# A Perceiver block with its second cross-attention rebuilt around 32x32 block transposes and row tiles

## The chip, the cores and the metric

The kernel runs on one core of one Trainium2 chip. The metric is the device time of one execution in microseconds (us). A profiled execution gives the trace, whose rows are quoted below: PE is TensorE's matmul side, PEld its weight loads, DVE VectorE, ACT ScalarE, POOL GpSimd, SP SyncE, and "SPq" rows are instructions of SP's own stream, which issues every DMA of this kernel.

## The reference, cut to what matters

Six stages are applied in turn to x of shape 64 x 32 x 128: cross-attention, memory attention, experts, a second cross-attention, a recurrent block and a quantised feed-forward block. The change touches the fourth, and what the third prepares for it:

```python
x = x + _L1_xattn_ref(ctx_1024, _layernorm(x), mask, Wq, Wkv, Wout, bout, g_media, b_media, g_latent, b_latent)

xn = layer_norm(ctx, g_media, b_media)        # 64 x 257 x 128
ln = layer_norm(latents, g_latent, b_latent)  # 64 x 32 x 128
kv_input = concatenate([xn, ln], axis=1)      # 289 keys a batch
sim = einsum('bhqd,bhfd->bhqf', q, k)         # 16 heads, 32 queries
sim = where(mask, max_neg, sim)
out = einsum('bhqf,bhfv->bhqv', softmax(sim), v) @ Wout + bout
```

## The kernel before

All is f32, and tokens lie as columns (128 features on the partitions) unless said otherwise. The weights are folded: `wqk` (16 heads of 128x128) turns a latent into a query that is multiplied with the normed key input itself, and `wvo` takes the mean of key inputs to the output. So the second cross-attention needs, for each of 64 batches, the 289 key inputs once as columns (`keyT`, for the scores) and once as rows (for the means).

**experts_0.** Besides 8 experts on 2048 tokens it norms the context. Its work is a loop of 32 units in 4 turns of 8. In unit s, PE does `up` (4 matmuls of 512 columns, L1085), `turn` of the context tiles of unit s-2 (4 transposes, L1107) and `down` of unit s-1 (16 matmuls, L1094). VectorE does, in this order, `measure` (4 BN_STATS, L1180), `normalise` of the unit before (4 tensor_scalar, L1200), `gather` (4 BN_AGGR, L1189) and, once `down` is made, 4 sums into `acc` (L1219). PE's `turn` waits for `normed`, which `normalise` counts up. SP loads each pair of context batches into a ring of four slots, in 2 DMAs (L1032), when the slot has been turned; ScalarE applies gain and bias while it copies the turned tiles into `keyT` (L1154).

**cross_attention_1.** A unit is one group of 4 heads of one batch: 128 rows (4 heads x 32 queries) by 289 keys; 4 units are a batch, 256 units in all. Per batch SP copies the key columns to a buffer (L1291) and loads the mask row (L1292), and PE turns the key columns into rows with 3 transposes (L1321), which VectorE copies (L1446). Per unit:

```python
nc.tensor.matmul(S[u % 2], q..., key[:, b % 2, 0:KEYS], start=True, stop=False)           # L1344
nc.tensor.matmul(S[u % 2][:, 0:CTX], lowest[:], maskb[:, b % 2, :], start=False, ...)     # L1345
nc.vector.tensor_reduce(nmax..., S[u % 2], AXX, ALU.max, negate=True)                     # L1472
nc.scalar.activation(P..., S[u % 2], ACT.Exp, bias=nmax..., accum_out=total...)           # L1426
nc.vector.tensor_scalar(P..., P..., rtotal..., None, ALU.mult)                            # L1452
nc.tensor.transpose(TP[u % 2]..., P[:, u % 4, ...], core.ident[:])                        # L1353, 3 of them
nc.scalar.activation(pT..., TP[u % 2], ACT.Copy)                                          # L1418
nc.tensor.matmul(OP..., xv[:, b % 2, k, :], pT[:, u % 2, k, :], ...)                      # L1364, k in 0..2
```

The queries of the next four batches (L1331, 16 matmuls, copied by ScalarE at L1411) and the projection of the last four (L1373, 16 matmuls) are spread or placed among the units. An f32 matmul appears in the trace as two passes with a weight load each; a transpose as one pass. A matmul of 4 independent tiles of 32 rows stands in the first cross-attention: its scores (L373) multiply 32 rows by 32 rows for 4 groups of heads, each into a bank of its own. That stage also has the mask and maximum in one VectorE instruction (L470), and the kernel's only 32x32 block transposes (L515).

## Time and profile before

| | us |
|---|---|
| median of 3 runs (lowest, highest) | 1561.96 (1558.83, 1562.1) |
| the profiled execution, own time | 1562.48 |
| its span, first to last instruction | 1560.7 |
| PE busy in the span | 1362.0 |
| VectorE / ScalarE / GpSimd busy | 851.6 / 804.3 / 146.0 |
| mean granted TensorE clock | 0.919 of full speed |

The span is what the trace covers; the profiled execution took 1.78 us more. Busy time is a mean over stages that have different limits, so a stage is read by its own stretch of the trace: the experts' loop from about 464 to 727 us and the second cross-attention from about 754 to 1318 us.

### The profile page before, as it was taken

How to read it: one execution, taken by the hardware profiler on the slowest of the kernel's cores; microseconds unless marked ns; L12 is line 12 of the kernel's file. 1: busy time of each engine (PE TensorE's matmuls, PEld its weight loads, DVE VectorE, ACT ScalarE, POOL GpSimd, SP SyncE). 2: the span in 40 equal slices, each digit the busy share in tenths (PEclk: the TensorE clock that was granted, in tenths of full speed). 3: DMA queues.
4: the chain of work that ended last, by engine and by line, in shares of the span. 5: the costliest groups of instructions: out<-in, count | busy, mean ns of one | idle time of the engine just before them, and what ended most of it. 6: DMA issues, size and time to landing. Idle time of an engine off the chain costs nothing. (4 is left out here: it accounts for less than half of the span.)

```text
span 1560.7 us, 36610 instructions
## 1 busy us (share of the span) xinstructions
PE 1362.0 (87%) x12406; PEld 1038.3 (67%) x12406; DVE 851.6 (55%) x2728; ACT 804.3 (52%) x1838; POOL 146.0 (9%) x432
## 2 busy tenths in 40 slices
PE   5799999666759999997899999999999999577855
PEld 2677777366536777775688888888888887212433
DVE  3466666478433444444555555555555554654387
ACT  3588888278314444442555555455555554444423
POOL 0122221364001111110000000000000000000000
PEclk8899999899669999997999999999999999787965
DMA  3332331000012111110000000000000000000000
GB/s 96 89 75 73 76 74 50 1 0 0 0 52 86 55 55 47 48 41 0 20 17 16 21 15 19 15 19 15 19 15 19 15 21 4 1 0 1 20 1 27
DMA packets 58225, 47.58 MB, mean 30 GB/s; under 512 B 11048, under 2 KB 55600, under 8 KB 58032
## 3 DMA queue, kind: packets, MB, share of 16 engines
q1 hardware_dynamic: 58160, 46.74, 10.9%
q8 instruction: 37, 0.61, 0.2%
q14 instruction: 28, 0.23, 0.0%
HBM read 36.07 MB, written 1.18 MB: 24 GB/s over the span
## 5 line engine op out<-in xcount | busy, mean ns | idle before, releaser
L1426 ACT ACTIVATE d_p<-bank,d_nmax 128x289 f32<-128x289 f32 x256 | 128.8, 503 | 239.0 <-DVE d_nmax L1472 238.9
L1364 PE MATMUL bank<-d_pT,d_xv 128*128 128x128 f32 x1536 | 220.3, 280 | 0.1
L1472 DVE TENSOR_REDUCE d_nmax<-bank 128x1 f32<-128x289 f32 x256 | 116.7, 456 | 171.3 <-PE bank L1345 169.6
L1364 PEld LDWEIGHTS bank<-d_pT,d_xv 128*128 128x128 f32 x1536 | 191.3, 191 | 12.1 <-ACT d_pT L1418 6.3
L1344 PE MATMUL bank<-d_key,d_q 128*128 128x289 f32 x512 | 167.3, 408 | 0.6 <-ACT d_q L1411 0.4
L1162 ACT ACTIVATE c_hs<-bank,c_w 128x512 f32<-128x512 f32 x128 | 87.8, 687 | 147.1 <-PE bank L1085 145.6
L431 ACT ACTIVATE a_p<-a_p,a_nmax 128x257 f32<-128x257 f32 x256 | 115.5, 500 | 38.6 <-DVE a_nmax L470 38.5
L1353 PE MATMUL bank<-ident,d_p 128*128 128x128 f32 x768 | 125.9, 273 | 0.1
L1418 ACT ACTIVATE d_pT<-bank 128x384 f32<-128x384 f32 x256 | 123.0, 480 | 0.9 <-PE bank L1353 0.8
L1085 PE MATMUL bank<-yT,c_w 128*128 128x512 f32 x256 | 118.2, 606 | 6.0 <-DMA c_w<-in_L_ffn_w 6.0
L1094 PE MATMUL bank<-c_w,c_hs 128*128 128x128 f32 x1024 | 122.0, 278 | 0.0
L1094 PEld LDWEIGHTS bank<-c_w,c_hs 128*128 128x128 f32 x1024 | 119.3, 195 | 0.1
L1353 PEld LDWEIGHTS bank<-ident,d_p 128*128 128x128 f32 x768 | 91.4, 141 | 38.2 <-DVE d_p L1452 6.1
L1219 DVE SCALAR_TENSOR_TENSOR c_acc<-bank,c_gates,c_acc 128x128 f32<-128x128 f32 x128 | 36.0, 344 | 142.6 <-PE bank L1094 142.6
L470 DVE CUSTOM_DVE_ANT_0 a_p<-bank,a_low 128x257 f32<-128x257 f32 x256 | 93.6, 422 | 28.1 <-PE bank L373 27.6
L1452 DVE TENSOR_SCALAR d_p<-d_p,d_rtotal 128x289 f32<-128x289 f32 x256 | 95.3, 372 | 9.1
L1085 PEld LDWEIGHTS bank<-yT,c_w 128*128 128x128 f32 x256 | 47.4, 195 | 54.6 <-issue 48.1
L1344 PEld LDWEIGHTS bank<-d_key,d_q 128*128 128x128 f32 x512 | 77.7, 192 | 1.2 <-ACT d_q L1411 0.6
L1331 PE MATMUL bank<-d_latT,x_wqk 128*128 (+1 forms) x512 | 68.6, 279 | 3.8 <-POOL d_lowest L1309 3.8
L1345 PE MATMUL bank<-d_maskb,d_lowest 128*128 128x257 bf16 x256 | 70.0, 274 | 0.0
L438 ACT ACTIVATE a_pT<-bank 128x512 f32<-128x512 f32 x128 | 68.5, 583 | 2.2 <-PE bank L383 2.2
L383 PE MATMUL bank<-ident,a_p 128*128 128x128 f32 x512 | 69.1, 280 | 0.0
(268 smaller groups left out, 2304.6 us busy)
## 6 DMA issues: line engine op xcount, KB each, us to landing
d_key<-x_keyT SPq DMA_DIRECT2D x64, 144.5 KB
a_ctT<-in_ctxT SPq DMA_DIRECT2D x64, 128.5 KB, 2.1
a_low<-mask_low SPq DMA_DIRECT2D x64, 128.5 KB, 3.0
c_ct<-in_ctx SPq DMA_DIRECT2D x64, 128.0 KB, 2.2
c_w<-in_L_ffn_w SPq DMA_DIRECT2D x8, 514.0 KB, 3.8
xT<-in_xT SPq DMA_DIRECT2D x4, 256.0 KB, 3.5
a_vlast<-values_last SPq DMA_DIRECT2D x4, 256.0 KB, 6.4
d_maskb<-mask_bf SPq DMA_DIRECT2D x64, 0.5 KB
```

Source lines behind the costliest of these rows:

```text
L431: nc.scalar.activation(P[:, r % 2, g, :], P[:, r % 2, g, :], ACT.Exp, bias=nmax[:, r % 2, g:g + 1], scale=-1.0).then_inc(exp_made, 1)
L470: nc.vector.tensor_tensor_reduce(P[:, r % 2, g, :], S[g], low[:, r % RING, :], -1.0, 3.4e38, ALU.add, ALU.min, accum_out=nmax[:, r % 2, g: ...
L1085: nc.tensor.matmul(UP[k], w[:, j, 128 * k:128 * k + 128], chunk(core.yT, c), start=True, stop=True).then_inc(up_made, 1)
L1094: ins = nc.tensor.matmul(Y[s % 2][:, m, :], hs[:, s % 2, k, 128 * m:128 * m + 128], w[:, j, HID + 128 * k:HID + 128 * k + 128], start=(k = ...
L1162: nc.scalar.activation(hs[:, s % 2, k, :], UP[k], ACT.Relu, bias=w[:, s // NCH, 2 * HID + k:2 * HID + k + 1]).then_inc(relu_made, 1)
L1344: nc.tensor.matmul(S[u % 2], q[:, half, b, 4 * g:4 * g + 4, :].rearrange("p h q -> p (h q)"), key[:, b % 2, 0:KEYS], start=True, stop=False)
L1353: ins = nc.tensor.transpose(TP[u % 2][:, 128 * k:128 * k + 128], P[:, u % 4, 128 * k:128 * k + 128], core.ident[:])
L1364: ins = nc.tensor.matmul(OP[:, 128 * g:128 * g + 128], xv[:, b % 2, k, :], pT[:, u % 2, k, :], start=(k == 0), stop=(k == 2))
L1418: nc.scalar.activation(pT[:, u % 2].rearrange("p k q -> p (k q)"), TP[u % 2], ACT.Copy).then_inc(t_copied, 1)
L1426: nc.scalar.activation(P[:, u % 4, 0:KEYS], S[u % 2], ACT.Exp, bias=nmax[:, u % 4:u % 4 + 1], accum_out=total[:, u % 4:u % 4 + 1]).then_in ...
L1452: nc.vector.tensor_scalar(P[:, u % 4, 0:KEYS], P[:, u % 4, 0:KEYS], rtotal[:, u % 4:u % 4 + 1], None, ALU.mult).then_inc(normed, 1)
L1472: nc.vector.tensor_reduce(nmax[:, u % 4:u % 4 + 1], S[u % 2], AXX, ALU.max, negate=True).then_inc(max_made, 1)
```

## The change

Four things are changed together.

- **Probabilities.** VectorE turns them in 32x32 blocks (128x320, 10 blocks of 32 keys), so block k of head j has its 32 keys on partitions 32j to 32j+31. PE's transposes and ScalarE's copies go. GpSimd, idle there before, multiplies by the inverse total. Mask, maximum and the move out of PSUM are one VectorE instruction, as in the first cross-attention; the mask matmul goes, and scores read `keyT` itself.
- **Means.** For each block of 32 keys, 4 matmuls of 32 rows (one for each head of a group, all 4 groups in its 128 columns), each into its own bank: 40 a batch instead of 12. Each of the four row groups needs the same key rows, which SP loads from memory 4 times a batch.
- **Key rows.** They come back from memory, so experts_0 must put them there with gain and bias applied: `normalise` gets a second pass of 4 instructions, and each pair of batches is loaded in 8 DMAs and stored in 8, by the partition order that the blocks want. Latents are turned at the start of the second cross-attention and stored too.
- **Order.** Queries and projection are spread evenly, one fourth a batch; queries have one PSUM bank instead of two.

```diff
+        self.low_dram = core.nc.dram_tensor("mask1_low", (BATCH, CTX + LAT), F32, kind="Internal").ap()
+        self.rows_dram = core.nc.dram_tensor("key_rows", (BATCH, 32, 10, 128), F32, kind="Internal").ap()
+        self.rows_stored = [core.sem(f"x_rows_stored{n}") for n in range(5)]
...
                 def load_pair(i, s):
                     for b in range(2):
-                        rows = t["ctx"][bass.ds((i * (2 * UNITS) + (2 * s + b)) * CTX, 256), :].rearrange("(k p) d -> p k d", p=128)
-                        sp.dma_start(ct[:, s % RING, 2 * b:2 * b + 2, :], rows).then_inc(ct_loaded[s % RING], 16)
+                        rows = t["ctx"][bass.ds((i * (2 * UNITS) + (2 * s + b)) * CTX, 256), :].rearrange("(k r a) d -> a k r d", k=32, a=4)
+                        for a in range(4):
+                            sp.dma_start(ct[32 * a:32 * a + 32, s % RING, 2 * b:2 * b + 2, :], rows[a]).then_inc(ct_loaded[s % RING], 16)
+
+                def store_pair(i, s):
+                    sp.wait_ge(normed, i * UNITS + (s + 2))
+                    for b in range(2):
+                        rows = cx.rows_dram[bass.ds(i * (2 * UNITS) + (2 * s + b), 1), :, 0:8, :].rearrange("b k (r a) d -> a (b k) r d", a=4)
+                        for a in range(4):
+                            sp.dma_start(rows[a], ct[32 * a:32 * a + 32, s % RING, 2 * b:2 * b + 2, :]).then_inc(cx.rows_stored[s % RING], 16)
...
+                def next_pair(i, s):
+
+                    store_pair(i, s - 3)
+                    sp.wait_ge(turned, i * UNITS + (s - RING + 2))
+                    sp.wait_ge(cx.rows_stored[s % RING], (i * 2 + s // RING) * 128)
+                    load_pair(i, s)
...
-                    sp.wait_ge(turned, s - RING + 2)
-                    load_pair(0, s)
+                    next_pair(0, s)
...
-                        ins = nc.vector.tensor_scalar(ct[0:rows, at, m, :], ct[0:rows, at, m, :], moments[0:rows, at, m, 0:1],
-                                                      rstd[0:rows, at, m:m + 1], ALU.subtract, ALU.mult)
+                        ins = nc.vector.scalar_tensor_tensor(ct[0:rows, at, m, :], ct[0:rows, at, m, :], moments[0:rows, at, m, 0:1],
+                                                             cx.media[0:rows, 0, :], ALU.subtract, ALU.mult)
+                    ins.then_inc(centred, 1)
+                    dve.wait_ge(centred, i * UNITS + (s + 2))
+                    for m in range(tiles):
+                        ins = nc.vector.scalar_tensor_tensor(ct[0:rows, at, m, :], ct[0:rows, at, m, :], rstd[0:rows, at, m:m + 1],
+                                                             cx.media[0:rows, 1, :], ALU.mult, ALU.add)
...
-                    sp.dma_start(key[:, b % 2, 0:KEYS], keyT[:, bass.ds(n, 1), :].rearrange("p a k -> p (a k)")).then_inc(key_loaded[b % 2], 16)
-                    sp.dma_start(maskb[0:1, b % 2, :], cx.mask_dram[bass.ds(n, 1), :]).then_inc(key_loaded[b % 2], 16)
+                        sp.wait_ge(max_made, (n - 3) * GROUPS)
+                    sp.dma_start(low[:, b % 4, :], cx.low_dram[bass.ds(n, 1), :].broadcast_to([128, KEYS])).then_inc(low_loaded[b % 4], 16)
...
+                def rows(i, b, first=False):
+
+                    n = i * EIGHT + b
+                    if not first:
+                        sp.wait_ge(o_made, n - 1)
+                    for j in range(4):
+                        sp.dma_start(xr[32 * j:32 * j + 32, b % 2, 0:BLOCKS - 1, :].rearrange("p r d -> p (r d)"),
+                                     cx.rows_dram[bass.ds(n, 1), :, 0:BLOCKS - 1, :].rearrange("b k r d -> (b k) (r d)")).then_inc(xr_loaded[b % 2], 16)
+                    for j in range(4):
+                        sp.dma_start(xr[32 * j:32 * j + 1, b % 2, BLOCKS - 1, :],
+                                     cx.rows_dram[bass.ds(n, 1), 0, BLOCKS - 1, :]).then_inc(xr_loaded[b % 2], 16)
...
+                def normalise(i, u):
+                    b, g = divmod(u, GROUPS)
+                    pool.wait_ge(recip, i * UNITS + (u + 1))
+                    p = P[:, b % 2, g, 0:KEYS]
+                    nc.gpsimd.tensor_tensor(p, p, rtotal[:, b % 2, g:g + 1].broadcast_to([128, KEYS]), ALU.mult).then_inc(normed, 1)
...
+                def queries(i, b):
+
+                    r, ahead = b % 4, b // 4 + 1
+                    if not (isinstance(i, int) and (i * 2 + ahead) * 4 + r == 0):
+                        pe.wait_ge(q_copied, (i * 2 + ahead) * 4 + r)
...
+                        pe.wait_ge(max_made, i * UNITS + (u - 1))
+                    nc.tensor.matmul(S[u % 2], q[:, b // 4, b % 4, 4 * g:4 * g + 4, :].rearrange("p h q -> p (h q)"),
+                                     keyT[:, bass.ds(i * EIGHT + b, 1), :].rearrange("p a k -> p (a k)"), start=True, stop=True).then_inc(s_made, 1)
...
+                def means(i, b, first=False):
+
+                    n = i * EIGHT + b
+                    pe.wait_ge(xr_loaded[b % 2], (i * (EIGHT // 2) + b // 2) * 128 + 128)
+                    pe.wait_ge(turned, (n + 1) * GROUPS)
+                    if not first:
+                        pe.wait_ge(o_copied, n)
+                    for k in range(BLOCKS):
+                        for j in range(4):
+                            rows = slice(32 * j, 32 * j + 32)
+                            ins = nc.tensor.matmul(O[j], xr[rows, b % 2, k, :], pT[rows, b % 2, :, 32 * k:32 * k + 32], start=(k == 0), stop=(k == BLOCKS - 1))
+                    ins.then_inc(o_made, 1)
...
+                def body(i, first, last):
+                    for b in range(EIGHT):
+                        scores(i, b, 0, first)
+                        scores(i, b, 1, first)
+                        if not (last and b >= 4):
+                            queries(i, b)
+                        scores(i, b, 2, first)
+                        scores(i, b, 3, first)
+                        if not (first and b < 5):
+                            project(i, b)
                         if not (first and b == 0):
-                            pe.wait_ge(o_copied, i * 8 + b)
-                    pe.wait_ge(t_copied, i * UNITS + (u + 1))
-                    for k in range(3):
-                        ins = nc.tensor.matmul(OP[:, 128 * g:128 * g + 128], xv[:, b % 2, k, :], pT[:, u % 2, k, :],
-                                               start=(k == 0), stop=(k == 2))
-                    ins.then_inc(o_made, 1)
-
-                def project(i, g):
-
-
-                    pe.wait_ge(o_copied, (i * 2 + g + 1) * 4)
-                    for h in range(HEADS):
-                        ins = nc.tensor.matmul(OUT, wvo[:, h, :], a[:, :, h, :], start=(h == 0), stop=(h == HEADS - 1))
-                    ins.then_inc(out_made, 1)
-
-                pe.wait_ge(low_made, 2)
-                pe.wait_ge(padded, 3)
+                            means(i, b - 1, first and b == 1)
...
+                    nc.vector.nop(nofuse=True)
+                    nc.vector.tensor_tensor_reduce(P[:, b % 2, g, 0:KEYS], S[u % 2], low[:, b % 4, :], -1.0, 3.4e38, ALU.add, ALU.min,
+                                                   accum_out=nmax[:, b % 2, g:g + 1]).then_inc(max_made, 1)
...
+                def turn(i, u, first=False):
+
+                    b, g = divmod(u, GROUPS)
+                    dve.wait_ge(normed, i * UNITS + (u + 1))
+                    if g == 0 and not (first and b < 2):
+                        dve.wait_ge(o_made, i * EIGHT + (b - 1))
+                    nc.vector.transpose(pT[:, b % 2, g, :], P[:, b % 2, g, :]).then_inc(turned, 1)
...
+                        maximum(i, u, first)
                         if not (first and u < 1):
-                            normalise(i, u - 1)
-                        if u % 4 == 2:
-                            if not (first and u == 2):
-                                means(i, u // 4 - 1, first)
-                            if not (last and u // 4 == 7):
-                                key_rows(i, u // 4 + 1, first and u < 4)
-                        if v == 5 and not (first and half == 0):
-                            project(i, half - 1)
-
-                nc.vector.memset(key[:, :, KEYS:WIDE], 0.0).then_inc(padded, 1)
-                nc.vector.memset(P[:, :, KEYS:WIDE], 0.0).then_inc(padded, 1)
-                key_rows(0, 0, True)
+                            invert(i, u - 1)
+                        if not (first and u < 2):
+                            turn(i, u - 2, first)
+                        if b % 4 == 1 and g == 1 and not first:
+                            project(i, (b - 9) // 4)
```

On PE, in the second cross-attention, this stood for a batch before: the key transposes and then four times scores (`d_key`), mask (`d_maskb`), transposes (`d_p`) and means (`d_xv`); two of the four units are shown.

```order
L1344 MATMUL bank<-d_key,d_q 128x289
L1345 MATMUL bank<-d_maskb,d_lowest 128x257
L1353 MATMUL bank<-ident,d_p 128x128 x3
L1364 MATMUL bank<-d_pT,d_xv 128x128 x3
L1321 MATMUL bank<-ident,d_key 128x128 x3
L1344 MATMUL bank<-d_key,d_q 128x289
L1345 MATMUL bank<-d_maskb,d_lowest 128x257
L1353 MATMUL bank<-ident,d_p 128x128 x3
L1364 MATMUL bank<-d_pT,d_xv 128x128 x3
```

Now one batch, with its fourth of the queries (`x_wqk`) and of the projection (`x_wvo`), and the means of the batch before (`d_xr`):

```order
L1387 MATMUL bank<-x_keyT,d_q 128x289 x2
L1377 MATMUL bank<-yT,x_wqk 128x128 x4
L1387 MATMUL bank<-x_keyT,d_q 128x289 x2
L1412 MATMUL bank<-d_a,x_wvo 128x128 x4
L1400 MATMUL bank<-d_pT,d_xr 128x128 x40
```

What moved: per unit only the scores are left, and all the means of a batch stand behind them as one run of 40.

On SP, the first issues of the experts' stage before (`c_ct` are context tiles, the last row is 4 pairs):

```order
L1027 DMA c_w<-in_L_ffn_w 128x1028
L1035 DMA c_ct<-in_ctx_last 64x128
L1032 DMA c_ct<-in_ctx 128x2x128 x8
L1027 DMA c_w<-in_L_ffn_w 128x1028
L1040 DMA x_wqT<-in_L_xattn_WqT 128x1024
L1040 DMA x_wkT<-in_L_xattn_WkT 128x1024
L1040 DMA x_wvT<-in_L_xattn_WvT 128x1024
L1040 DMA x_wout<-in_L_xattn_Wout 128x1024
L1042 DMA mask_bf<-x_mask 64x257
L1032 DMA c_ct<-in_ctx 128x2x128 x8
```

The same place now, up to the load of the fifth pair:

```order
L1044 DMA c_ct<-in_ctx 32x2x128 x32
L1038 DMA c_w<-in_L_ffn_w 128x1028
L1066 DMA c_wqT<-in_L_xattn_WqT 128x1024
L1066 DMA c_wkT<-in_L_xattn_WkT 128x1024
L1066 DMA c_wvT<-in_L_xattn_WvT 128x1024
L1066 DMA c_wout<-in_L_xattn_Wout 128x1024
L1068 DMA mask_low<-x_low 64x289
L1070 DMA key_rows<-c_ct 64x128
L1051 DMA key_rows<-c_ct 32x2x128 x16
L1044 DMA c_ct<-in_ctx 32x2x128 x8
```

What moved: a pair that was 2 issues is 16, 8 out of the slot's `c_ct` to `key_rows` and 8 into it. In the loop of turns 1 to 3 each of them has a register instruction ahead of it, as each c_ct load had before.

On VectorE, one unit of the experts' loop before:

```order
L1180 BN_STATS c_stats<-c_ct 128x6 x4
L1200 TENSOR_SCALAR c_ct<-c_ct,c_moments,c_rstd 128x128 x4
L1189 BN_AGGR c_moments<-c_stats 128x2 x4
L1219 SCALAR_TENSOR_TENSOR c_acc<-bank,c_gates,c_acc 128x128 x4
L1180 BN_STATS c_stats<-c_ct 128x6 x4
```

and now:

```order
L1208 BN_STATS c_stats<-c_ct 128x6 x4
L1228 SCALAR_TENSOR_TENSOR c_ct<-c_ct,c_moments,x_media 128x128 x4
L1233 SCALAR_TENSOR_TENSOR c_ct<-c_ct,c_rstd,x_media 128x128 x4
L1217 BN_AGGR c_moments<-c_stats 128x2 x4
L1252 SCALAR_TENSOR_TENSOR c_acc<-bank,c_gates,c_acc 128x128 x4
```

What moved: between the statistics (`c_stats`) of one unit and the sums (`c_acc`) of the same unit stand 8 instructions on `c_ct` instead of 4, the second four behind a wait for the first.

## Rows read from the trace of the kernel before

**Rows 1.** Busy time in two stretches: length, each engine, granted clock, DMA share, GB/s.

```profile
480.00:700.00 220.00, 219.83 (x1283) 157.46 (x1282) 97.81 (x475) 101.64 (x148) 34.95 (x58) 1.00 0.17 48
765.00:1300.00 535.00, 535.00 (x4108) 474.14 (x4109) 293.52 (x878) 276.06 (x801) 0.00 (x0) 1.00 0.05 18
```

**Rows 2.** Timeline, PE, second cross-attention: start, us, line, tiles, passes.

```profile
1000.06 0.83 PE L1364 MATMUL bank<-d_pT,d_xv 128*128 128x128 f32 x6
...
1000.73 0.65 PE L1344 MATMUL bank<-d_key,d_q 128*128 128x289 f32 x2
...
1001.22 0.27 PE L1345 MATMUL bank<-d_maskb,d_lowest 128*128 128x257 bf16 x1
...
1001.33 0.49 PE L1353 MATMUL bank<-ident,d_p 128*128 128x128 f32 x3
...
1001.66 0.28 PE L1364 MATMUL bank<-d_pT,d_xv 128*128 128x128 f32 x1
```

**Rows 3.** Timeline, SP, second cross-attention: first and last of nine copies, eight batches apart.

```profile
883.41 0.50 SPq L1291 DMA_DIRECT2D d_key<-x_keyT  x1
...
953.14 0.49 SPq L1291 DMA_DIRECT2D d_key<-x_keyT  x1
```

**Rows 4.** Groups by line, PE, first cross-attention: busy us, mean ns, idle before.

```profile
L373 PE MATMUL bank<-a_kT,a_qb 32*128 32x257 f32 x512 | 51.9, 440 | 3.0 <-issue 2.3 <-DVE a_nmax L470 0.7
...
L354 PE MATMUL bank<-a_ctT,wa_wk 128*128 128x257 f32 x128 | 46.1, 443 | 9.1 <-DMA a_ctT<-in_ctxT 9.1
```

**Rows 5.** Timeline, PE, 182.13 to 182.37 us: a full-array pass, then row tiles.

```profile
182.14 0.28 PE L362 MATMUL bank<-wa_wv,a_ctT 128*128 128x128 f32 x1
182.34 0.50 PE L373 MATMUL bank<-a_kT,a_qb 32*128 32x257 f32 x4
```

**Rows 6.** Timeline, experts' loop: two units' sums, and one unit between.

```profile
606.77 1.13 DVE L1219 SCALAR_TENSOR_TENSOR c_acc<-bank,c_gates,c_acc 128x128 f32<-128x128 f32 x4 [4.23 <-PE bank L1094]
...
614.35 1.13 DVE L1219 SCALAR_TENSOR_TENSOR c_acc<-bank,c_gates,c_acc 128x128 f32<-128x128 f32 x4 [4.23 <-PE bank L1094]
...
616.29 1.11 DVE L1200 TENSOR_SCALAR c_ct<-c_ct,c_moments,c_rstd 128x128 f32<-128x128 f32 x4
...
617.45 0.42 PEld L1107 LDWEIGHTS bank<-ident,c_ct 128*128 128x128 f32 x4 [0.74 <-DVE c_ct L1200]
```

**Rows 7.** Timeline, SP, experts' loop: the two issues of one pair.

```profile
618.30 0.37 SPq L1032 DMA_DIRECT2D c_ct<-in_ctx  x1
...
618.87 0.37 SPq L1032 DMA_DIRECT2D c_ct<-in_ctx  x1
```

**Rows 8.** One line each: count, ns min/median/max, first and last start, form.

```profile
L1292 SPq DMA_DIRECT2D d_maskb<-mask_bf x64: 278/286/442, 757.0 to 1295.4; - x64
L1291 SPq DMA_DIRECT2D d_key<-x_keyT x64: 491/492/545, 756.4 to 1294.7; - x64
L515 DVE STREAM_TRANSPOSE a_oT<-a_orow x4: 669/670/711, 275.8 to 277.6; 128x512 f32<-128x512 f32 x4
L470 DVE CUSTOM_DVE_ANT_0 a_p<-bank,a_low x256: 418/421/430, 32.9 to 269.3; 128x257 f32<-128x257 f32 x128
L323 POOL TENSOR_TENSOR a_qb<-a_qT,a_own_head x64: 397/399/402, 26.6 to 264.1; 128x128 f32<-128x128 f32 x64
L331 POOL TENSOR_TENSOR a_edge<-a_vlast,a_p x64: 243/244/248, 40.9 to 270.5; 128x32 f32<-128x32 f32 x64
```

**Rows 9.** The page, DMA issues: KB each, median us from issue to landing.

```profile
c_ct<-in_ctx SPq DMA_DIRECT2D x64, 128.0 KB, 2.2
```

**Rows 10.** Busy time in stretches with idle gaps on PE; columns as in rows 1.

```profile
340.00:390.00 50.00, 35.20 (x293) 33.06 (x292) 40.86 (x63) 41.35 (x118) 23.20 (x64) 1.00 0.00 0
704.00:708.00 4.00, 0.78 (x5) 0.76 (x5) 3.30 (x16) 0.00 (x0) 0.36 (x2) 0.77 0.00 0
```

**Rows 11.** Timeline, PE, start of the second cross-attention: queries, then the first scores.

```profile
754.54 5.20 PE L1331 MATMUL bank<-d_latT,x_wqk 128*128 128x128 f32 x32 [3.83 <-POOL d_lowest L1309]
...
760.43 0.76 PE L1344 MATMUL bank<-d_key,d_q 128*128 128x289 f32 x2 [0.36 <-ACT d_q L1411]
```

More of the change, by code:

```diff
@@ L17 @@
 EPS = 1e-5
+LOWEST = -3.3895313892515355e38
 class Core:
@@ L1299, in _ @@
+                sp.wait_ge(lat_stored, NCH * 16)
+                for b in range(EIGHT):
+                    if b >= 4:
+                        mask(0, b)
+                    rows(0, b, b < 2)
                 with sp.Fori(1, TURNS) as i:
-                    for b in range(8):
-                        load(i, b)
+                    for b in range(EIGHT):
+                        mask(i, b)
+                        rows(i, b)
             @block.gpsimd
             def _(pool):
-                nc.gpsimd.memset(lowest[:], 0.0).then_inc(low_made, 1)
@@ new lines, in project @@
+                def project(i, b):
+                    ago, r = divmod(b - 5, 4)
+                    if r == 0:
+                        pe.wait_ge(o_copied, (i * 2 + ago + 1) * 4)
+                        if not (isinstance(i, int) and i * 2 + ago == 0):
+                            pe.wait_ge(out_added, i * 2 + ago)
+                    for h in range(4 * r, 4 * r + 4):
+                        ins = nc.tensor.matmul(OUT, wvo[:, h, :], a[:, ago % 2, h].rearrange("p b q -> p (b q)"), start=(h == 0), stop=(h == HEADS - 1))
+                    if r == 3:
+                        ins.then_inc(out_made, 1)
@@ L1397, in _ @@
+                for m in range(TILES):
+                    ins = nc.tensor.transpose(core.bank[:, 2 + m // 4, 128 * (m % 4):128 * (m % 4) + 128], latT[:, 128 * m:128 * m + 128], core.ident[:])
+                    if m % 4 == 3:
+                        ins.then_inc(lat_turned, 1)
+                for r in range(4):
+                    queries(-1, 4 + r)
+                pe.wait_ge(latents_placed, 1)
+                pe.wait_ge(lat_kept, NCH)
                 peeled(pe, TURNS, body)
-                transposes(TURNS, -2)
@@ L1433, in _ @@
+                def body(i, first, last):
+                    for b in range(EIGHT):
+                        for g in range(GROUPS):
+                            exponential(i, b * GROUPS + g)
+                        if not (last and b >= 4):
+                            queries(i, b)
+                        if not (first and b == 0):
+                            means(i, b - 1, first)
                 for r in range(4):
-                    queries(0, 0, r)
+                    queries(-1, 4 + r)
```

274 lines of the change are left out of this document (117 added, 157 removed).

## Prediction, made before the changed kernel ran

> **What bounds the kernel now.** The changed lines run in two loops, so I read the stretches of these loops first. In both, PE is busy all the time at the full clock: 219.83 of 220 us in the experts' loop, all of 535 us in the second cross-attention, where VectorE is busy for 293.52 and ScalarE for 276.06 [rows 1]. So PE's passes are what an edit there must shorten. The second view is PE's own timeline, read by its starts, since the ends overlap. Six passes of the means take 1000.73 - 1000.06 = 0.67 us, so a pass of 128 columns costs 0.112; the scores take 0.49 (two passes of 289 columns), the mask matmul 0.11 and three transposes 0.33 [rows 2]. That is 1.60 a unit, with no gap. The third view is SP's timeline: nine key copies lie eight batches apart, (953.14 - 883.41) / 8 = 8.72 us a batch [rows 3], 558 for 64.
>
> In the experts' loop busy PE misleads. A unit takes 614.35 - 606.77 = 7.58 us, and once in each PE's weight loads sit idle for 0.74 until VectorE's `normalise` is through [rows 6]. The cycle is: `down` is made, VectorE sums, measures and normalises, only then `turn` and the next `down` follow on PE. Whatever makes `normalise` longer makes the unit longer. This decides half of the answer.
>
> **The second cross-attention.** What goes, per batch: 4 x 0.67 for the means, 4 x 0.33 for transposes, 4 x 0.11 for masks, and 0.33 for the key transposes (three passes like those of a unit). That is 4.77, and 8.72 - 4.77 = 3.95 stay (scores, queries, projection, small waits). What comes is 40 matmuls, 80 passes, in 20 quads of four row tiles. No quad of 128 columns stands in the trace. The nearest rows are the scores of the first cross-attention: 512 passes of 32 rows are busy for 51.9 us, so a batch's 8 passes for 0.81, while 2 full-array passes of the same 257 columns are busy for 46.1 / 64 = 0.72 [rows 4]. Four tiles cost about what one costs. All four first passes start within 0.03 us [rows 5]. So I take a full-array pass for a quad: 20 x 0.112 = 2.24. The bounds: below, nothing less than that, as the columns have to stream. Above, a quad that hides neither its weight load nor the tiles behind each other: 80 x 0.112 = 8.96.
>
> Entering row tiles is not free. The last full pass starts at 182.14 and would give way at 182.25; the tiles' load starts at 182.34, and it has no matmul to hide behind, which I put at one more pass, 0.11 [rows 5]. That is 0.20 an entry. I take the same for the way back, which no row shows apart (bounds 0 and 0.20), so 0.40 a batch. The Trainium skill (TensorEngine Tiling (Array Packing), Key Properties) states that changing the tiling mode drains TensorE; the trace agrees with its 0.09 us before the load.
>
> So a batch becomes 3.95 + 2.24 + 0.40 = 6.59, and 64 x (8.72 - 6.59) = **136 us less**.
>
> Does another engine take over at 6.6 us? VectorE per unit: the masked maximum on 289 columns (0.42 at 257 columns, so about 0.45, with its accumulator read within 0.6), the reciprocal that was there before, and a block transpose of 320 columns, which lies between 0.42 (the 0.67 of 512 columns by columns) and 0.67 [rows 8]. That is 1.1 to 1.4, or 4.4 to 5.6 a batch. GpSimd's multiply of 289 columns, from 0.244 for 32 columns and 0.398 for 128 (1.6 ns a column) is 0.66, or 2.6 a batch [rows 8]. ScalarE loses four copies a batch and gains one. SP has 9 issues a batch, at about 0.53 each (below), 4.8. PE stays last. The wait of the means for the last block transpose: it is behind the second maximum of the next batch on VectorE, near 2.9 us after that batch's first scores (scores 0.49, maximum 0.6, reciprocal, transpose, maximum, transpose at about 0.5 each), while PE comes to the means after 3.95 - so it is covered by 1.0 us. The key rows may be reloaded when the means two batches before are made; 8 issues of 0.53 and a landing of 2.2 [rows 9] are 6.4 against 6.6 + 3.9. If that cover went, PE would wait for the rest.
>
> The start gets longer. Before, 32 passes of queries take 5.20, then come the scores, at 760.43 - 754.54 = 5.9 [rows 11]. Now 16 transposes of latents go first (at the same 0.163 a pass: 2.6), and each of the four query groups waits for ScalarE to empty the one bank, about 1 us, three times. I put 5 us; the bound above is 8, as the key rows are needed a whole batch later. The end (projection after the last means) keeps its form.
>
> **The experts' loop.** `normalise` gets four more instructions in front of `turn`. The four there take 1.11 for a last duration of 0.34, so the starts are 0.26 apart [rows 6]; four more are 1.04, and the wait for `centred` exposes the end of the fourth, 0.11. So 1.15 a unit: 31 units give 36, and the last `normalise`, which stands alone, 1. Nothing covers it, since PE waits there already. The bound below is 0.4 less a unit if PE's idle 0.74 held slack that I don't see. The unit becomes 8.73.
>
> SP's stream is the second term. Two issues of a pair start 0.57 apart, of which 0.37 is the issue and 0.20 the registers [rows 7]. An issue of one run takes 0.286, one of the 256 runs here 0.37, and the copy out of SBUF 0.492 [rows 8]. Mine move 64 runs, half of them out of SBUF: I take 0.33, so 0.53 each, 16 of them 8.5, and 8.8 with the expert weights and waits. The bounds are 16 x 0.49 = 7.8 and 16 x 0.69 = 11.1. At 8.8 SP is just the slower one in the 24 units of turns 1 to 3: 24 x 0.1, about 3 us. Then PE idles some 1.8 us a unit. Where it idled for most of 704 to 708 us, the granted clock fell to 0.77 there; with 35.20 busy of 50 us in shorter gaps it held at 1.00 [rows 10]. I take 4 us for some falls. Experts: 36 + 1 + 3 + 4 = **44 us more**.
>
> **The sum.** 1562.5 (own time of the profiled execution, 0.5 above the median of its three runs) - 136 + 5 + 44 = 1475.5, so 1475 for the median. A measurement of this kernel tells about 0.2%, 3 us, from no change.
>
> **The rivals.**
> - *Quads overlap only in part.* For it: in rows 4 the busy time is a union of modelled ends, and means accumulate over ten quads without a break, which no row shows. With a quad at 1.3 passes, 20 x 0.034 x 64 = 43 us come back: about 1519. The Trainium skill (TensorE: Matmul & The Clock Gate, Measured speedup vs the span model) gives 3.07 times for four row tiles of 512 columns; by it the estimate is a quad of 4 / 3.07 passes, the same 1519. The 0.81 against 0.72 of rows 4 speaks for 1.13, about 1494. Chance 0.14.
> - *Each quad pays load and stream in turn: slower.* The place is the run of 40 matmuls. The gain left is 87 us, 1.36 a batch, 0.068 for each of 20 quads: from 0.180 a quad on the kernel is slower. If the load of the next block can't go behind the running quad, a quad is 0.22, the batch 2.2 longer, and the time 1475 + 141 = 1616. Against it: in rows 4 the second passes hide their loads. Chance 0.07.
> - *SP bounds the experts' loop.* If every small issue costs what the copy out of SBUF does, a unit is 11.1 + 0.3, that is 2.6 more over 24 units, 62: about 1537. Idle gaps of 4 us a unit on PE would then cost clock, and half clock on a few us of each unit leads to 1580 at worst. Chance 0.17.
> - *Cheaper than I think:* no cost for leaving row tiles, and part of `normalise` in slack, 13 + 12 us: 1450. Chance 0.09.
> - *The forecast:* 0.53, its own range 1457 to 1500.
>
> **How the numbers follow.** The range leaves out the serial quads and the worst of SP, and reaches to 1443 and 1548. Faster: the forecast, the partial overlap, the cheap case and nearly all of SP's, 0.91; I keep 0.02 for no change and 0.07 for slower, the second rival.
>
> **What would show it.** In the profile after: key-row means as x80 passes a batch, 20 starts of four at 0.11 apart; a batch at 6.6 between mask loads on SP; VectorE under 5.6 a batch; the experts' sums 8.7 to 8.9 apart, with PE waiting for VectorE's second `normalise` and not for a DMA; SP issues at 0.53. It is wrong if the quads start more than 0.15 apart, if VectorE waits for `c_ct` loads in turns 1 to 3, or if the clock in the experts' loop is well under 1.

## The result, and the profile after

| | before | after |
|---|---|---|
| median (lowest, highest), us | 1560.98 (1558.83, 1562.1) | 1598.4 (1595.49, 1601.08) |
| span of the profiled execution | 1560.7 | 1596.7 |
| mean granted TensorE clock | 0.919 | 0.882 |

After to before is 1.0227, with a 95% interval of 1.0193 to 1.0261. The change costs 37 us where 86 less were forecast, and 1598 lies outside the range of 1443 to 1548.

The stretches come first, as in [rows 1]. The columns are the stretch, busy time and instructions of PE, PEld, DVE, ACT and POOL, the granted clock, the DMA share and GB/s. This is the changed kernel in turns 1 to 3 of the experts' loop, and in eight batches of the second cross-attention:

```profile
545.00:850.00 305.00, 203.12 (x1077) 140.66 (x1078) 107.61 (x480) 80.25 (x121) 28.92 (x48) 0.84 0.19 52
1009.70:1067.70 58.00, 53.09 (x833) 46.54 (x832) 29.58 (x131) 28.76 (x80) 21.24 (x33) 0.97 0.40 105
```

PE was busy all the time in both loops before. Now it idles for a third of the experts' loop, at a mean clock of 0.84, and for 5 us in each eight batches of the other. The waits of the changed kernel between 545 and 850 us name what it idles for (engine and line, what it waited for, us in total, times, longest):

```profile
PE bank L1114 <- DMA c_w<-in_L_ffn_w: 89.9, 6, 16.6
PEld bank L1114 <- DMA c_w<-in_L_ffn_w: 31.6, 2, 16.4
```

`c_w` holds the weights of an expert, which the change doesn't touch. Six times, once per switch of expert (PE goes on to the weights of the next one), `up` waits for them. The kernel before has no such wait in this loop. SP's timeline (start, duration, instruction, count) around one switch shows why:

```profile
584.89 3.88 SPq L1051 DMA_DIRECT2D key_rows<-c_ct  x8
589.07 5.84 SPq L1044 DMA_DIRECT2D c_ct<-in_ctx  x8
595.10 0.44 SPq L1038 DMA_DIRECT2D c_w<-in_L_ffn_w  x1
595.79 3.82 SPq L1051 DMA_DIRECT2D key_rows<-c_ct  x8
...
614.42 4.18 SPq L1051 DMA_DIRECT2D key_rows<-c_ct  x8
```

and PE's timeline for the same time:

```profile
583.74 0.50 PE L1123 MATMUL bank<-c_w,c_hs 128*128 128x128 f32 x3
599.01 6.49 PE L1114 MATMUL bank<-yT,c_w 128*128 128x512 f32 x8 [14.77 <-DMA c_w<-in_L_ffn_w]
605.33 0.60 PE L1136 MATMUL bank<-ident,c_ct 128*128 128x128 f32 x4
605.77 3.74 PE L1123 MATMUL bank<-c_w,c_hs 128*128 128x128 f32 x32
609.34 3.60 PE L1114 MATMUL bank<-yT,c_w 128*128 128x512 f32 x8
614.32 0.66 PE L1136 MATMUL bank<-ident,c_ct 128*128 128x128 f32 x4 [1.38 <-DVE c_ct L1233]
```

PE is out of work at 584.24. SP issues the weights only at 595.10, behind 16 issues of a pair, and `up` begins 3.9 us later. The eight passes of this `up` take 6.49 us, the next eight 3.60: after the idle time the first ones run at the lower of the clock's two levels (1.2 GHz, not 2.4). These are the stretch after this gap and the one after the gap at 1004.22 that is shown below, columns as above, with a granted clock of 0.50:

```profile
599.00:602.00 3.00, 2.99 (x4) 1.45 (x5) 0.00 (x0) 0.69 (x1) 0.00 (x0) 0.50 0.19 49
1004.20:1006.50 2.30, 2.28 (x5) 1.71 (x6) 0.81 (x4) 0.31 (x1) 0.19 (x1) 0.50 0.32 59
```

The wait at 614.32 is the longer `normalise`, as forecast. So between switches a unit takes 8.6 to 8.9 us, mostly 8.65 (sums of successive units start so far apart), and the six units at a switch take 25.0, 25.5, 25.9, 23.7, 25.9 and 24.9: 150.9 - 6 x 8.65 = 99 us of gaps.

In the second cross-attention the quads do what the prediction took for them, and a new gap stands between turns. PE's timeline of the changed kernel across a jump back of its loop:

```profile
996.22 1.05 PE L1412 MATMUL bank<-d_a,x_wvo 128*128 128x128 f32 x8
997.20 2.51 PE L1400 MATMUL bank<-d_pT,d_xr 32*128 32x128 f32 x80
1004.22 2.29 PE L1387 MATMUL bank<-x_keyT,d_q 128*128 x4 [4.51 <-issue]
...
1009.70 2.51 PE L1400 MATMUL bank<-d_pT,d_xr 32*128 32x128 f32 x80
1012.14 1.24 PE L1387 MATMUL bank<-x_keyT,d_q 128*128 x4
```

From the means to the scores behind them 2.44 us pass: 20 quads (a quad is four passes of 32 rows side by side) at 0.112, 0.10 more in the first, and 0.11 for leaving the tiles. Five times, once per eight batches, the scores come only after 7.02 us, and the row says "issue": PE waited for nothing that the profile shows. The four passes behind the gap take 2.29 us, not 1.24, which is the lower clock.

The 36.0 us between the spans, by starts of rows (before, after):

| part | forecast | measured |
|---|---|---|
| experts, first to last sum: 478.6 to 715.0, 481.2 to 852.9 | +44 | +135.3 |
| last sum to first means: 764.95 and 909.26 | +5 | +6.4 |
| first to last means: to 1312.47 and 1346.61 | -136 | -110.2 |
| ahead of the first sum and behind the last means | 0 | +4.5 |

### The profile page after: what moved, and what is told of

Same layout as the page of the kernel before. It is cut to its first block and busy times, and to the rows that moved or that the text cites. A ratio compares the mean times of both kernels' runs of the same rounds, so it can differ in the third digit from the quotient of the medians.

```text
span 1596.7 us, 43594 instructions
## 1 busy us (share of the span) xinstructions
PE 1252.3 (78%) x14790; PEld 918.4 (58%) x14790; DVE 822.1 (51%) x2987; ACT 742.9 (47%) x1646; POOL 316.0 (20%) x687
## 5 line engine op out<-in xcount | busy, mean ns | idle before, releaser
L1357 POOL TENSOR_TENSOR d_p<-d_p,d_rtotal 128x289 f32<-128x289 f32 x256 | 170.3, 665 | 279.3 <-DVE d_rtotal L1498 279.3
L1492 DVE CUSTOM_DVE_ANT_0 d_p<-bank,d_low 128x289 f32<-128x289 f32 x256 | 112.1, 438 | 210.7 <-PE bank L1387 178.9
L1457 ACT ACTIVATE d_p<-d_p,d_nmax 128x289 f32<-128x289 f32 x256 | 137.7, 538 | 134.4 <-DVE d_nmax L1492 134.3
L1387 PE MATMUL bank<-x_keyT,d_q 128*128 (+1 forms) x512 | 162.6, 437 | 26.6 <-issue 22.6
L1400 PE MATMUL bank<-d_pT,d_xr 32*128 32x128 f32 x5120 | 160.9, 275 | 0.0
L1400 PEld LDWEIGHTS bank<-d_pT,d_xr 32*128 32x128 f32 x5120 | 148.7, 187 | 8.8 <-issue 1.5
L1506 DVE STREAM_TRANSPOSE d_pT<-d_p 128x320 f32<-128x320 f32 x256 | 128.4, 502 | 1.9 <-POOL d_p L1357 1.1
L1387 PEld LDWEIGHTS bank<-x_keyT,d_q 128*128 128x128 f32 x512 | 87.2, 195 | 58.4 <-issue 24.5
L1377 PEld LDWEIGHTS bank<-yT,x_wqk 128*128 128x128 f32 x512 | 70.7, 201 | 10.7 <-ACT d_q L1450 3.5
L1377 PE MATMUL bank<-yT,x_wqk 128*128 (+1 forms) x512 | 70.9, 284 | 2.4 <-ACT d_q L1450 2.4
```

The source lines that it names most:

```text
L1357: nc.gpsimd.tensor_tensor(p, p, rtotal[:, b % 2, g:g + 1].broadcast_to([128, KEYS]), ALU.mult).then_inc(normed, 1)
L1377: ins = nc.tensor.matmul(Q[:, 128 * h:128 * h + 128], wqk[:, 4 * r + h, :], latT[:, bass.ds((i * 2 + ahead) * 128, 128)], start=True, stop ...
L1387: nc.tensor.matmul(S[u % 2], q[:, b // 4, b % 4, 4 * g:4 * g + 4, :].rearrange("p h q -> p (h q)"), keyT[:, bass.ds(i * EIGHT + b, 1), :]. ...
L1400: ins = nc.tensor.matmul(O[j], xr[rows, b % 2, k, :], pT[rows, b % 2, :, 32 * k:32 * k + 32], start=(k == 0), stop=(k == BLOCKS - 1))
L1457: nc.scalar.activation(p, p, ACT.Exp, bias=nmax[:, b % 2, g:g + 1], scale=-1.0, accum_out=total[:, b % 2, g:g + 1]).then_inc(exp_made, 1)
L1492: nc.vector.tensor_tensor_reduce(P[:, b % 2, g, 0:KEYS], S[u % 2], low[:, b % 4, :], -1.0, 3.4e38, ALU.add, ALU.min, accum_out=nmax[:, b % ...
```

## The experiments

**Theory**, from the profile after: the loss sits in SP's one queue. Its 16 issues a unit put the weights far back in its order (it is late), they also take longer than a unit (it is too slow). In the fourth stage each jump back of PE's long loop body costs 6 us. **Rivals:** the stores' traffic delays landings; VectorE's longer `normalise` holds most of the loss; the key rows come late at the start of a turn. Times of experiments stand beside runs of the kernel before on the same chip; the ratio is to those, with its 95% interval. Where a time is set against the changed kernel, the two ran on different chips, on which the medians of the kernel before lie between 1560.2 and 1564.2 us.

### The order in SP's queue

`e1_weights_earlier` moves one issue past eight others:

```diff
                     sp.wait_ge(cx.rows_stored[s % RING], (i * 2 + s // RING) * 128)
+                    if weights:                       # s % NCH == 0
+                        load(i, s // NCH)
                     load_pair(i, s)
...
-                        if s % NCH == 1:
-                            sp.wait_ge(down_made, i * UNITS + NCH * (s // NCH - 1))
-                            load(i, s // NCH)
```

> The load of the expert weights is issued eight DMA issues earlier in SP's order (behind the stores of the same pair, before its loads); nothing else changes. Theory (SP's queue is late, so the weights are issued late): of the six stretches in which PE waits 15 to 16 us for c_w, each gets shorter by the 5.9 us that eight load issues take (589.07 to 595.10 in the profile after); 6 x 5.9 = 35, and one more period of four units may follow, so 1598 - 35 = about 1563 (1555 to 1568), and the issue of c_w comes 5.9 us closer to the last sum before it. Rival (the weights land late because stores and loads share the DMA engines): the issue moves, the landing does not, and the time stays at 1595 to 1600. Rival (VectorE's longer normalise sets the stage): no change either, since VectorE's work is the same.

Measured: 1556.44 us, ratio 0.9973 (0.9954 to 0.9992), 42 less than the changed kernel. The six long units are now 16.6, 18.1, 21.0, 17.5, 19.3 and 18.0 us. One issue in another place takes the whole loss back, with the same bytes, the same count of issues and the same work of VectorE. Both rivals predicted no change here. The edit also drops SP's wait for `down_made`. That it matters isn't to be seen: in the changed kernel between 545 and 850 us the only wait of SP in the profile is that of the stores for `normalise`.

`e7_weights_ahead` goes further: the weights of the next expert are issued in the middle of the last pair ahead of the switch (`if b == 1 and weights is not None: load(*weights)` in `load_pair`), and the last turn is written out.

> All 16 issues of a pair stay on SP, but the next expert's weights are issued a whole unit and more earlier, between the loads of the last pair before the switch (their buffer is free by then). Theory (two faults of one queue: it is late, and it is too slow): with the lateness gone the throughput of SP is left, 16 issues of 0.66 us, about 10.8 us for each of 24 units of turns 1 to 3, spread evenly, PE waiting for the rows' normalise and VectorE for the loads of c_ct instead of PE for c_w: from the first sum to the last 60 + 24 x 10.85 + 11 = 332 us instead of 372, so about 1558 (1550 to 1562), no better than the run with the weights eight issues earlier. Rival (only the lateness counts, the queue is fast enough): units of 8.65 and 1498 to 1504.

Measured: 1537.51 us, ratio 0.9843 (0.9807 to 0.9878). The waits for `c_w` shrink to 8.6 us in all, and units of turns 1 to 3 take 8.6 to 15.7 us, 10.5 on average. So the queue is also too slow, as the theory said, but I had the size too high, and 1537.5 lies below the range of 1550 to 1562. First to last sum is 314.4 us, not 332: the 332 counted one unit too many (31 intervals, not 32, 8.7 us), and 24 units at 10.5 instead of 10.85 are the other 9. SP's timeline in this kernel:

```profile
657.11 3.87 SPq L1053 DMA_DIRECT2D key_rows<-c_ct  x8
661.24 2.85 SPq L1046 DMA_DIRECT2D c_ct<-in_ctx  x4
664.29 0.42 SPq L1038 DMA_DIRECT2D c_w<-in_L_ffn_w  x1
664.95 3.19 SPq L1046 DMA_DIRECT2D c_ct<-in_ctx  x4
668.39 3.87 SPq L1053 DMA_DIRECT2D key_rows<-c_ct  x8
```

One pair takes 668.39 - 657.11 = 11.3 us with a load of weights in it, 10.2 to 10.8 without. In the last turn, which this edit writes out, pairs take 8.9 to 10.2. SP waits for nothing in these turns by the profile, so its own issuing is the limit. Now it is VectorE that waits for its rows:

```profile
DVE c_stats L1217 <- DMA c_ct<-in_ctx: 27.2, 16, 4.6
```

### The number of issues

`e3_stores_on_scalar` lets ScalarE issue the stores (`act.dma_start` behind `keep`, the same addresses).

> The eight stores of a pair are issued by ScalarE behind its copy of the turned keys, not by SP; the same bytes move. Theory (SP's 16 issues of about 0.66 us, 10.7 us a unit against a unit of 8.65, make the weights late): SP has 5.9 us a unit left, c_w is there in time, all units take 8.65, and the six gaps of 14.6 to 16.9 us (97 in all) go: 1598 - 97 = 1501. ScalarE's own load of eight issues, some 4 us a unit beside 3.4 us of work, could lengthen a unit by up to 0.8 us: 1501 to 1526. Rival (traffic of the stores delays landings): the gaps stay, 1595 or more. Rival (VectorE): no change.

Measured: 1524.77 us, ratio 0.9772 (0.9727 to 0.9818), inside the theory's range, but partly by luck: the range reached that far for a ScalarE that lengthens every unit, while units between switches stay at 8.65 to 8.85 and the six at a switch take 12.9 to 14.8, with PE still waiting for `c_w`. The same bytes are stored, and PE's waits for `c_w` are down from 13.1 to 16.6 us each to 4.4 at the longest, so their traffic is not what held the weights.

`e4_four_issues` gives the rows of a pair to partitions so that two neighbours share one, and a batch needs one DMA each way:

```diff
-                        rows = t["ctx"][...].rearrange("(k r a) d -> a k r d", k=32, a=4)
-                        for a in range(4):
-                            sp.dma_start(ct[32 * a:32 * a + 32, s % RING, 2 * b:2 * b + 2, :], rows[a])...
+                        rows = t["ctx"][...].rearrange("(p r) d -> p r d", r=2)
+                        sp.dma_start(ct[:, s % RING, 2 * b:2 * b + 2, :], rows)...
...
-  nc.tensor.matmul(O[j], xr[rows, b % 2, k, :], ...)
+  nc.tensor.matmul(O[j], xr[rows, b % 2, 2 * (k % 4) + k // 4 if k < 8 else k, :], ...)
```

The stores are changed alike, and the mask is laid out in the new order of keys.

> Rows of a pair are given to partitions so that a batch's 256 rows are loaded with one DMA and stored with one (partition 32j+t holds rows 64j+2t and 64j+2t+1): 4 issues a unit instead of 16, the same bytes, mask and means in the same order of rows. Theory (number of issues on SP): SP needs about 2 us a unit, no wait for c_w, 32 units of 8.65, the six gaps of 97 us in all go: 1598 - 97 = 1501 (1494 to 1508), and the granted clock between 520 and 850 us is back at 1.00. Rival (bytes and traffic): no change, 1595 to 1600. Rival (VectorE's longer normalise holds most of the loss): no change.

Measured: 1519.9 us, ratio 0.975 (0.9705 to 0.9795). A step of 78 us, but 19 short of what I expected: the six units at the switches still take 12.7, 11.4, 11.2, 11.3, 13.8 and 12.7. SP's timeline and then PE's, both of this kernel, show what is left:

```profile
603.06 1.37 SPq L1049 DMA_DIRECT2D key_rows<-c_ct  x2
604.80 0.89 SPq L1043 DMA_DIRECT2D c_ct<-in_ctx  x2
606.00 0.33 SPq L1038 DMA_DIRECT2D c_w<-in_L_ffn_w  x1
```

```profile
602.92 0.66 PE L1134 MATMUL bank<-ident,c_ct 128*128 128x128 f32 x4 [1.03 <-DVE c_ct L1231]
603.41 3.74 PE L1121 MATMUL bank<-c_w,c_hs 128*128 128x128 f32 x32
610.65 3.69 PE L1112 MATMUL bank<-yT,c_w 128*128 128x512 f32 x8 [3.50 <-DMA c_w<-in_L_ffn_w]
```

SP is idle until 603.06, when `normalise` of a pair is through (PE's transposes of it begin at 602.92). Only then do its stores go out, and behind them the weights, which PE needs at 607.1. So there is a second part of the lateness that fewer issues don't cure: the weights stand behind a wait that the change put there, on a pair one younger than the one SP waited for before (`turned` of pair s-4 then, `normed` of pair s-3 now).

`e8_four_issues_ahead` is this kernel with the weights issued as in `e7`.

> Four issues a unit as before, and the weights issued between the loads of the last pair before the switch, no longer behind the stores that wait for normalise. Theory (what was left, 2.4 to 5.1 us at each of the six switches, is that the weights stand behind a store that waits for the normalise of a pair, and so come 3.8 us of landing after it): the six longer units become 8.65, that is (12.7 + 11.0 + 11.2 + 11.2 + 13.8 + 12.7) - 6 x 8.65 = 20.7 us less: 1520 - 21 = 1499 (1495 to 1503), no wait of PE for c_w. Rival (PE's jump back or the cold clock makes the first unit of an expert long): the time stays at 1517 to 1522.

Measured: 1499.24 us, ratio 0.9599 (0.9563 to 0.9635), and every unit of turns 1 to 3 takes 8.6 to 9.1 us. Against `e7` that is 38 us: the price of the slow queue once the weights are in time. The two differ in the number and shape of the issues. Faster transfers are not the reason, since the larger ones land later (`c_ct` 3.7 us after its issue in the median, against 2.1).

### VectorE's part

`e5_one_pass` puts the old `normalise` into the changed kernel and leaves gain and bias of the key rows out.

> The changed kernel with the old normalise of four instructions in the experts' loop (gain and bias of the key rows are left out). It asks how much of the loss in that loop is VectorE's. Theory (SP's lateness sets turns 1 to 3; VectorE's time stands in the chain from the landing of c_w to the next one only once or twice per four units): the first seven units and the last shorten by 1.15 each, 9 us, and each of six periods by 1.15 to 2.3, 7 to 14 us: 1598 - 20 = 1578 (1574 to 1583), the waits for c_w get longer, not shorter. Rival (each unit's length counts): 32 x 1.15 = 37 less, 1561.

Measured: 1577.99 us, ratio 1.0102 (1.0066 to 1.0138). The units between switches in turns 1 to 3 are back at 7.5 to 7.9 us, and the long ones take 24.2 to 28.4, up to 19.0 of it waiting for `c_w` (16.6 at the most in the changed kernel). So 16 of the 36 us that VectorE saves are lost again. While the queue is late, VectorE's 36 us are worth 20.

`e9_turn_behind_down` is `e8` with two calls of PE in the other order:

```diff
                         up(i, s, first)
-                        if not (first and s < 1):
-                            turn(i, s - 2, first)
                         if not (first and s == 0):
                             down(i, s - 1, first and s < 3)
+                        if not (first and s < 1):
+                            turn(i, s - 2, first)
```

> As the run with four issues and the weights ahead, and on PE the transposes of a pair stand behind down of the unit instead of ahead of it. Theory (a unit is 8.65 because turn waits for sum, measure and normalise on VectorE, 4.4 us, with only up, 3.6 us, to cover them): covered by up and down together, 7.3 us, the wait goes and a unit is PE's own 7.5: 31 x 1.15 = 36 less than 1499, 1463 (1458 to 1470). Rival (VectorE's chain with GpSimd's root and ScalarE's copies bounds the unit wherever turn stands): 8.65 stays, 1499.

Measured: 1460.5 us, ratio 0.934 (0.9302 to 0.9378). PE's timeline in this kernel has no wait left in the loop, with all eight VectorE instructions of `normalise` in place:

```profile
606.88 3.60 PE L1121 MATMUL bank<-yT,c_w 128*128 128x512 f32 x8
610.32 3.73 PE L1130 MATMUL bank<-c_w,c_hs 128*128 128x128 f32 x32
613.89 0.60 PE L1143 MATMUL bank<-ident,c_ct 128*128 128x128 f32 x4
614.33 3.60 PE L1121 MATMUL bank<-yT,c_w 128*128 128x512 f32 x8
```

A unit is 614.33 - 606.88 = 7.45 us, all of it PE's.

`e12_before_turn_later` makes the same swap in the kernel before.

> The kernel before with turn behind down in the experts' loop and nothing else. PE is busy for 40.00 of 40 us there, so the place of turn hides nothing that is still open: the wait of the weight loads for normalise (0.74 a unit) is on the load only. Theory: no change, 1558 to 1563. Rival (the 0.74 is real time of PE): 31 x 0.1 to 31 x 0.7, 3 to 20 us less.

Measured: 1558.78 us, ratio 0.997 (0.9953 to 0.9987). First to last sum goes from 236.4 to 233.1 us, 0.1 a unit. That is the lower end of the rival, not the theory's nothing, though the time lies in both ranges: a little of the 0.74 was real. The order of `turn` was worth 3 us before, and with the longer `normalise` it is worth 39 (`e8` to `e9`).

### The gap between turns

`e6_straight_pe` writes PE's turns out:

```diff
-                peeled(pe, TURNS, body)
+                for i in range(TURNS):
+                    body(i, i == 0, i == TURNS - 1)
```

> In the second cross-attention PE's eight turns are written out in a row, without a loop; the other engines keep their loops. Theory (each jump back of PE's long loop body leaves it without instructions for 4.5 us, five times, and a batch across such a jump takes 12.5 instead of 6.45 us): 5 x 6.05 = 30 us less, 1568 (1562 to 1573), and no idle time put down to issue. Rival (the key rows or the mask of the first batch of a turn come late): the gaps stay and the time too, 1595 to 1600. Rival (straight code can't be brought in fast enough, 1700 instructions in 52 us): gaps spread over the batches, at or above 1598.

Measured: 1562.54 us, ratio 1.0009 (0.9986 to 1.0031), 36 less than the changed kernel. The means of successive batches start 6.4 to 6.8 us apart across all the former jumps (7.2 at the most), with the key rows and masks as they were, so it was the jump. From first to last means the gain is 32 us, as five jumps of 6 would give; the other 4 or so lie outside that stretch, where the two kernels are the same. `e11_half_means` asks whether the length of the loop body matters. It leaves out every second block of the means.

> The changed kernel with every second block of the means left out in the second cross-attention (20 matmuls a batch instead of 40; the means are then over half of the keys). It asks whether the 4.5 us without instructions at each jump back hang on the length of PE's loop body, which falls from 208 to 128 matmul and load instructions a batch. Theory (a body this long is fetched anew at each jump, a body about as long as that of the kernel before is not): no gap, a batch across the jump takes what the others take, 64 x 1.12 + 30 = 102 less: 1496. Rival (each jump back costs its 6 us whatever the length): 64 x 1.12 = 72 less: 1526, with five gaps. In both, the quads' cadence stays 0.112 and a batch falls to about 5.3 us if PE stays the bound; if VectorE's block transposes or SP's nine issues then bound it, a batch stays above 5.5.

Measured in one run: 1513.67 us. That lies halfway between the theory's 1496 and the rival's 1526, so the time alone decides nothing; the timeline does. No gap of 6 us is left, and no wait of PE put down to "issue" is longer than 0.2 us there: after the first batches, means start 5.3 to 6.2 us apart, and 7.0, 7.3 and 8.2 at three places, where PE waits for VectorE. A batch is 5.7 us on average, not 5.3: VectorE now waits 62.9 us for mask rows. The count of packets that fetch instructions says it most plainly. This row of the DMA view between 903 and 1250 us (packets, MB, share of 16 engines) is that of the changed kernel, then of the one without PE's loop, then of the short body:

```profile
q8 instruction: 51, 0.84, 1.1%
```

```profile
q8 instruction: 43, 0.70, 0.8%
```

```profile
q8 instruction: 10, 0.16, 0.2%
```

The same view of the kernel before has no such row at all in this window. So a body of 832 passes and as many weight loads [above: x833, x832 in 58 us] is fetched anew in each turn; one of 512 is not, nor was the one before, of 536. Straight code is fetched nearly as often, but PE shows no gap for it. The Trainium skill (Runtime: NRT & Kernel Launch, Instruction fetch mechanics) says that a taken branch to a target outside the fetched window stalls until the target has been fetched; the 4.51 us of "issue" and these packets agree with it. Where between 536 and 832 the limit lies no run shows.

### All of it together

> Four issues a unit, weights ahead, turn behind down, and PE's eight turns of the second cross-attention in a row without a loop. If the two parts of the loss are independent, the 36 us that the run without PE's loop gave (1598.4 to 1562.5) come off 1460.5: 1425 (1420 to 1432). Rival (the straight code's fetches disturb the row transfers once the stages before are faster): less than 25 us, 1436 or more.

Measured with `e10_all`: 1427.85 us (1424.03 to 1430.97), ratio 0.9132 (0.9108 to 0.9155). The theory's range was 1420 to 1432, so the parts add up. Against `e9` it is 32.7 less, where 36 were expected: the 30 of the five jumps and what two medians can differ by. Its stretches, as in the first fence above, show PE busy all the time in the experts' loop and 98.8% of it in the other, at the full clock in both:

```profile
545.00:700.00 155.00, 155.00 (x920) 115.32 (x919) 92.78 (x417) 69.32 (x104) 25.31 (x42) 1.00 0.29 89
909.00:1180.00 271.00, 267.85 (x4288) 229.95 (x4284) 152.18 (x670) 146.02 (x407) 109.76 (x165) 1.00 0.42 114
```

The steps from 1598.4: four issues 78.5, weights ahead 20.7, `turn` behind `down` 38.7, no loop on PE 32.7, each uncertain by some 3 us, since the runs were on different chips. The first two depend on their order: weights ahead by itself gives 60.9 (`e7`), four issues then 38.3.

## Why the prediction was wrong, by its own steps

Of the 123 us between the 1475 forecast and the result, 91 are in the experts' loop and 26 in the second cross-attention.

- **The second cross-attention: right, and its main doubt settled.** A quad was taken as one full-array pass, 0.112; it is 0.112 from quad to quad. Entering costs 0.09 before the first load and 0.10 in the first quad, leaving 0.11, 0.30 in all against 0.40. A batch is 6.49 (means of `e6`, 48 batches, (1267.7 - 956.1) / 48) against 6.59. The first two rivals fall: there is neither partial overlap nor a serial quad. The figure of the Trainium skill beside the first rival (TensorE: Matmul & The Clock Gate, Measured speedup vs the span model), 3.07 times for 512 columns, is not what these quads of 128 columns show; their rows give 4 in the run, and 8.96 / 2.54 = 3.5 with the way in and out.
- **What it left out there: 30 us.** Five jumps, at each of which a batch takes about 12.5 instead of 6.45: 6.05 us, of which 4.5 are the gap and the rest mostly the lower clock behind it. The prediction counted passes by time and never looked at how long the loop body became, from 536 passes to 832. The 110 us measured are 140 less these 30.
- **The start: right.** 5 taken. From the last sum to the first means it is 6.4 more; from the first transpose of latents to the first scores 901.95 - 891.15 = 10.8 us pass, against the 5.9 before.
- **`normalise`: right to 0.1 us.** 8.73 forecast, 8.65 to 8.85 measured, a wait of PE for VectorE's second `normalise` as described: 36 us.
- **The step that failed: "SP's stream is the second term".** It reads: 0.53 an issue, 16 of them 8.5, "and 8.8 with the expert weights and waits", so "24 x 0.1, about 3 us". Two things in it were wrong. The size: a store is 0.52 but a load 0.75 ((595.10 - 589.07) / 8), so 16 issues are 10.2 us, within the stated bounds, and more than a unit. And the kind: the step priced the queue by its throughput only, and put the expert weights into 0.3 us as if only their own issue counted. What was queued behind the 16 issues, and behind the new wait for `normed`, was the one transfer that PE cannot do without. Throughput alone would have given the 10.5 us a unit of `e7`; the four units from one switch to the next take 50 to 52 us, 12.8 a unit. The two faults work together in the six gaps of 99 us: earlier weights alone take back 61 (`e7`), fewer issues alone 78 (`e4`), both together 99 (`e8`), so the 99 can't be split between them. The step put all of it at 3. The prediction says what stands behind the means' wait for the last block transpose, and never what stands behind the stores' wait on SP.
- **The third rival** had the right place and the wrong mechanism: "SP bounds the experts' loop" was 62 us spread over 24 units, and the loop lost 99 in six gaps. That `e7` comes out at its 1537 is chance: `e7` holds the 30 us of the jumps as well.
- **The clock.** 4 us taken. It is part of the gaps: the six `up`s behind one take 5.3 to 6.8 us each instead of 3.60, 15 us more in all; PE's waits for `c_w` ahead of them are 90 us.
- **"What would make it wrong"** named the sign to look for, the clock well under 1 in the experts' loop; it was 0.84. That PE waits "not for a DMA" failed as well. Of the other two signs the quads more than 0.15 apart did not show, and VectorE waits for `c_ct` loads only three times between 545 and 850 us, 1.7 us in all.

Shown by runs: the place in the queue, the number of issues, the order of `turn` and `down`, the jump back and that it hangs on the body (by one run with a shorter one). Not shown: how much of the 99 us each of the queue's two faults has, from what length a body is fetched anew, and how much of `e8`'s gain over `e7` is the count of the issues and how much their shape.

## What to carry to other kernels

Before adding DMAs to a queue, write down everything that is issued on it in order, and for each the time at which its consumer needs it: most of the price of sixteen small issues came through the weight load that stood behind them. Put a load that a stage can't start without ahead of any wait for a younger result, and prefer few DMAs with more runs over many with few. When a matmul is split into tiles, count the instructions of the loop body as well as its time, and when VectorE's work grows, look at which of PE's pieces could stand between it and the one that waits for it.

## What the runs showed of the hardware that I had not expected

- Four row tiles of 32 rows with 128 columns, 20 quads in a row, cost one full-array pass each (0.112 us a quad), so tiling gives a factor of four inside the run. The way in and out adds 0.30 us to the run.
- A jump back to a PE loop body of 832 passes costs 4.5 us without an instruction (4.3 to 4.9), 6.05 in the period; bodies of 512 and 536 passes show none.
- A load issue of 32 partitions with two rows each takes SP 0.75 us in the loop, a store of the same shape 0.52, from start to start; in the last turn of `e7`, which is written out, 0.63 ((767.59 - 762.52) / 8) and 0.50 ((762.52 - 758.55) / 8).
